# Turned softmax blocks of a decoder layer: sixteen SBUF-to-SBUF moves per unit, or four stores to DRAM and one fetch

## The chip, the cores and the metric

One NeuronCore of one Trainium2 chip runs the whole layer. The metric is device time in microseconds (us) of one execution. Stages are found by their time from the start of the profiled span.

## What is computed

A post-norm decoder layer over x (32 sequences of 56 tokens, 256 features): self-attention, cross-attention over 1500 context rows of 128 features per sequence, and a mixture-of-experts feed-forward part. The change lies in cross-attention alone:

```python
q = (text_hidden @ Wq).reshape(B, T_text, N_HEADS, HEAD_DIM).transpose(0, 2, 1, 3)    # 16 heads of 128
k = (vision_tokens @ Wk) ...  ; v = (vision_tokens @ Wv) ...                          # 8 heads, repeated twice
scores = jnp.einsum('bhtd,bhsd->bhts', q, k) / scale      # here 16*56 = 896 rows by 1500 keys per sequence
attn = jax.nn.softmax(jnp.where(mask, scores, -jnp.inf), axis=-1)
out = jnp.einsum('bhts,bhsd->bhtd', attn, v)
return out.transpose(0, 2, 1, 3).reshape(B, T_text, N_HEADS * HEAD_DIM) @ Wo
```

All is float32. A float32 product is made of three matmuls on a rounded part and a rest (`_hi`, `_lo`), so each operand is split by a rounding copy (ScalarE) and a subtraction (VectorE or GpSimd).

## The kernel before, in words

Three stages follow each other: `phase_a` (self-attention and queries, up to about 200 us), `phase_b` (cross-attention, up to about 2020 us, line 650 on), `phase_c` (experts). Keys and values are folded into the query and output weights ahead, so in `phase_b` the context itself serves as keys (`cT_*`, 128 x 1500) and as values (`c_*`, 125 partitions of 12 rows).

A batch m is one of the 32 sequences. Its 896 rows are seven units of 128 rows. For each unit TensorE makes three score fills of 500 keys (L860 to L862), VectorE takes each fill into `p` with the mask and a running maximum (L1070, then L1079), ScalarE makes the exponentials of the unit (L977). To multiply by the values the probabilities must be turned, so that keys lie on partitions. This is done in two ways:
- the three odd units by TensorE: 12 steps, one per column group c: turn (L874), round (`p_round`, L960), rest (`p_rest`, L1095), weigh (`weigh_odd`, L893 to L895);
- the four even units by VectorE and DMA: `turn_blocks` (L1090) transposes a unit in blocks of 32 x 32 into `by_block` (two buffers, unit u uses u % 2), and `move_blocks` on SyncE's queue (L799 to L808) brings the blocks into `keyed`, where row 32 r + j holds the keys. A unit takes sixteen DMAs of 32 partitions x 1536 bytes, one for each pair (a, r) of a partition strip a of `by_block` and a partition strip r of `keyed`. Then come 12 steps in two halves of six (units 0 and 1, then 2 and 3): round (`keyed_round` on ScalarE, L970), rest (`keyed_rest` on GpSimd, L1247, written over `keyed`), weigh (`weigh_even`, L916 to L918).

The order of work is written out by hand. Every engine goes through the same step number n = 0 to 23 (`STEPS`) of each batch, and work of a later stage lags by a fixed number of steps. The points that matter: `turn_blocks` of units 0 to 3 at `BLOCKS_AT` = 5, 8, 13, 17; `keyed_round` at steps 19 to 30 (`EVEN_HI`), so that the first half begins at step 19 and the second at step 25, which is step 1 of the next batch; weighing of even units two steps later; odd units turned at steps 31 to 42, which are 7 to 18 of the next batch. Step n + 24 of batch m is step n of batch m + 1. Score banks, turn banks and `pT_hi` are three deep, so the engines can't run far apart. Every second batch also holds a projection of two sequences (L928, four steps) with a norm (`norm`, `norm_out`) and the store of `y2`.

Waits around the change: `keyed_round` waits at the start of each half for the DMAs of its two units; `turn_blocks(m, u)` waits until the DMAs of the unit that had the same `by_block` buffer have landed; the moves of units 0 and 2 wait until the half of `keyed` that they overwrite has been weighed (`pv_done`). SyncE's queue is in order and carries also the loads of q (`load_q`), of the context in both forms (`load_cT`, `load_c`), of the mask, and the residual and `y2`. ScalarE's queue carries `store_rden` (L984, the softmax denominators as single floats, at steps 16 and 26) and `load_rden` (L992, at steps 23 and 33), which waits for the former to land. `phase_c` writes over `by_block` and waits first for `attention.moved`.

Of the kernel before, what the change touches and what calls it, by code (L numbers as in the profile page):

```python
# [29 lines left out]
F32 = mybir.dt.float32  # L30
# [6 lines left out]
B, S, F = 32, 56, 256  # L37
# [13 lines left out]
QUADS = 4  # L51
ACROSS = 32 * CH
# [579 lines left out]
def phase_b(nc, D, semaphore, edge, opening, M_hi, M_lo, q_in, cT_in, ident, const_loaded):  # L632
    with ExitStack() as ctx:
        def sb(name, shape, dt=F32):
            edge[name] = -(-nc.sbuf_base // 32) * 32
            return ctx.enter_context(nc.sbuf_tensor("b_" + name, shape, dt))
# [5 lines left out]
        def sem(name):  # L642
            return semaphore("b_" + name)
# [11 lines left out]
        keyed = sb("keyed", [128, EVEN * QUADS, ACROSS])  # L655
# [3 lines left out]
        p = [None, sb("p1", [128, ODD, CTX])]  # L659
# [23 lines left out]
        by_block = sb("by_block", [128, 2, QUADS, CH, 32])  # L683
        p[0] = sb("p0", [128, EVEN_DEEP, CTX_PAD])
        edge["end"] = nc.sbuf_usable_end // 32 * 32
        half = nc.alloc_sbuf_tensor_at("b_half", [PAIR, 1], F32, offset=edge["end"])
# [9 lines left out]
        shift_done, exp_done = sem("shift_done"), sem("exp_done")  # L696
        turned, hi_done, lo_done, pv_done = sem("turned"), sem("hi_done"), sem("lo_done"), sem("pv_done")
        blocks_turned, keyed_lo_done, keyed_lo_last = sem("blocks_turned"), sem("keyed_lo_done"), sem("keyed_lo_last")
        keyed_loaded = [sem(f"keyed_loaded{u}") for u in range(EVEN)]
        rden_done, rden_stored, rden_loaded = sem("rden_done"), sem("rden_stored"), sem("rden_loaded")  # L700
        oT_done, oT_hi_done, oT_lo_done, proj_done = sem("oT_done"), sem("oT_hi_done"), sem("oT_lo_done"), sem("proj_done")
        z_done, stat_chain, var_done, rstd_done, y2_done = sem("z_done"), sem("stat_chain"), sem("var_done"), sem("rstd_done"), sem("y2_done")
# [8 lines left out]
        EVEN_HI = 19  # L711
        EVEN_PV, ODD_HI = EVEN_HI + 2, EVEN_HI + CH
        ODD_PV = ODD_HI + 2
        BLOCKS_AT = (5, 8, 13, 17)
        RDEN_AT, STORE_AT, LOAD_AT = (15, STEPS + 1), (16, STEPS + 2), (STEPS - 1, STEPS + 9)
        SCALE_AT = (EVEN_PV + CH - 1, ODD_PV + CH - 1)
        ROUND_AT, ROUND_REST_AT = SCALE_AT[1] + 1, SCALE_AT[1] + 2
# [1 line left out]
        CT_HI_AT, C_HI_AT, FIRST_SPLIT_AT = 4, 9, 12  # L719
        OT_OPS = 2  # L720
        TAIL = range(STEPS, ROUND_REST_AT + 1)
        MOVES = 16 * QUADS * QUADS
        ORDER = [(u, j) for u in range(EVEN) for j in range(FILLS)] + [
            (EVEN + u, j) for u, j in ((0, 0), (0, 1), (1, 0), (1, 1), (2, 0), (0, 2), (1, 2), (2, 1), (2, 2))]

# [33 lines left out]
        def row(m, u):  # L759

            return p[0][:, (EVEN * m + u) % EVEN_DEEP, :] if u < EVEN else p[1][:, u - EVEN, :]

        def whole(m):

            return STEPS * (m + 1)
# [3 lines left out]
        def keyed_part(tensor, half, first, count):  # L769


            return tensor[0:CK, GROUPS * half:GROUPS * (half + 1), 32 * first:32 * (first + count)]

        def by_blocks(ap, width):
            return ap.rearrange("p (g j) -> p g j", j=width)

        def sync(sp):
            def load_q(m):
                sp.wait_ge(q_split, 2 * m)
                sp.dma_start(q_in[:], D["q"][:, m]).then_inc(q_loaded, 16)  # L780

            def load_cT(m):
                sp.wait_ge(cT_lo_done, m)
                sp.dma_start(cT_in[:], D["ctxT"][m]).then_inc(cT_loaded, 16)

            def load_mask(m):
                if m:
                    sp.wait_ge(mask_ready, m)
                sp.dma_start(mask_in[:], D["mask"][m].partition_broadcast(128)).then_inc(mask_loaded, 16)

            def load_c(m):
                if m >= 2:
                    sp.wait_ge(pv_done, whole(m - 2))
                if m:
                    sp.wait_ge(c_loaded, 16 * m)
                sp.dma_start(c_raw[m % 2][:], D["ctx"][m]).then_inc(c_loaded, 16)

            def move_blocks(m, u):


                if m and u % 2 == 0:
                    sp.wait_ge(pv_done, STEPS * (m - 1) + CH // 2 * (u // 2 + 1))
                sp.wait_ge(blocks_turned, EVEN * m + u + 1)
                for a in range(QUADS):
                    for r in range(QUADS):
                        sp.dma_start(keyed[32 * r:32 * (r + 1), QUADS * u + a, :],  # L806
                                     by_block[32 * a:32 * (a + 1), u % 2, r].rearrange("q b j -> q (b j)")).then_inc(
                                         keyed_loaded[u], 16)  # L808

            def residual(i):  # L810

                sp.dma_start(z[:], D["y1"][:, i, :]).then_inc(res_loaded, 16)

            def store(i):
                sp.wait_ge(y2_done, i + 1)
                sp.dma_start(D["y2"][PAIR * i:PAIR * (i + 1), :], y2[:]).then_inc(y2_stored, 16)

            def load_ahead():
                load_mask(0)
                load_c(0)  # L820

            store_last_part, wait_stored = opening.sync(sp, load_ahead)
            load_q(1)
            load_cT(1)
            load_mask(1)
            for part in range(len(opening.stored)):
                store_last_part(part)
            wait_stored()
            residual(0)

            for m in range(B):
                move_blocks(m, 0)
                if m + 2 < B:
                    load_q(m + 2)
                move_blocks(m, 1)
                if m % 2 and m >= 3:
                    store((m - 3) // 2)
                    residual((m - 1) // 2)
                move_blocks(m, 2)
                if m + 2 < B:  # L840
                    load_cT(m + 2)
                    load_mask(m + 2)
                move_blocks(m, 3)
                if m < LAST:
                    load_c(m + 1)
            return lambda: store(END)
# [108 lines left out]
        def scalar(act):  # L955
# [6 lines left out]
            def keyed_round(m, s):  # L962

                n, half, pair = STEPS * m + s, s // (CH // 2), s % (CH // 2)
                if pair == 0:
                    for u in (2 * half, 2 * half + 1):
                        act.wait_ge(keyed_loaded[u], MOVES * (m + 1))
                if n >= 3:
                    act.wait_ge(pv_done, n - 2)
                act.copy(by_blocks(pT_hi[:, s % 3, :], 64), keyed_part(keyed, half, 2 * pair, 2)).then_inc(hi_done, 1)  # L970
# [45 lines left out]
            def lag_step(m, n):  # L1016
                if at := behind(m, n, ODD_HI, CH):
                    p_round(*at)
                if at := behind(m, n, EVEN_HI, CH):
                    keyed_round(*at)  # L1020
                for par in range(2):
                    if at := behind(m, n, LOAD_AT[par]):
                        load_rden(at[0], par)
                    if at := behind(m, n, STORE_AT[par]):
                        store_rden(at[0], par)
                if at := behind(m, n, ROUND_AT):
                    oT_round(at[0])
# [26 lines left out]
        def vector(dve):  # L1054
# [27 lines left out]
            def turn_blocks(m, u):  # L1082


                dve.wait_ge(exp_done, PUNITS * m + u + 1)
                if m or u >= 2:
                    dve.wait_ge(keyed_loaded[(u + 2) % EVEN], MOVES * (m + u // 2))
                own = row(m, u)
                keys = bass.AP(own.tensor, own.offset, [own.ap[0], [32, QUADS], [CK, CH], [1, 32]])
                dve.transpose(by_block[:, u % 2], keys).then_inc(blocks_turned, 1)  # L1090
# [92 lines left out]
            def block_step(m, n):  # L1183
                if n in BLOCKS_AT:
                    turn_blocks(m, BLOCKS_AT.index(n))

# [22 lines left out]
        def gpsimd(pool):  # L1209
# [60 lines left out]

        return Attention(
            sync, tensor, scalar, vector, gpsimd, edge, TAIL,
            q_split=(q_split, 2 * B), cT_split=(cT_lo_done, B),
            fill_done=(fill_done, PFILLS * B), fill_taken=(fill_taken, PFILLS * B),
            moved=[(loaded, MOVES * B) for loaded in keyed_loaded], rden_stored=(rden_stored, 32 * B),
            first_batch_weighed=(pv_done, whole(LAST - 1)), weighed=(pv_done, whole(LAST)),
            keyed_weighed=(pv_done, STEPS * LAST + CH), scaled=(oT_done, OT_OPS * 2 * B),
            projected=(proj_done, NPAIR), z_taken=(z_done, NPAIR), y2_stored=y2_stored)
# [931 lines left out]
def decoder_layer(nc, D):  # L2210
    with ExitStack() as ctx:
        def semaphore(name):
            return ctx.enter_context(nc.semaphore(name))

        with ExitStack() as memory:
            edge = {}

            def sb(name, shape, dt=F32):
                edge[name] = nc.sbuf_base
                return memory.enter_context(nc.sbuf_tensor(name, shape, dt))  # L2220

            ident_loaded = semaphore("ident_loaded")
            M_hi, M_lo = sb("M_hi", [128, XH, F], F32R), sb("M_lo", [128, XH, F], F32R)
            q_in, cT_in = sb("q_in", [128, ROWS]), sb("cT_in", [128, CTX])
            ident = sb("ident", [128, 128])
            opening = phase_a(nc, D, semaphore, M_hi, M_lo, q_in, cT_in, ident, ident_loaded)
            attention = phase_b(nc, D, semaphore, edge, opening, M_hi, M_lo, q_in, cT_in, ident, ident_loaded)
        phase_c(nc, D, semaphore, attention, ident)
# [68 lines left out]
```

## Time and profile before

| quantity | value |
|---|---|
| median of 2 runs | 2253.15 us (2252.69 to 2253.62) |
| the profiled execution | 2257.55 us, its span 2255.7 us |
| TensorE's mean granted clock over the span | 0.881 of full speed |
| busy over the span | PE 1710.5 us (76%), VectorE 1246.3 us (55%), ScalarE 1030.6 us (46%), GpSimd 1001.7 us (44%) |
| DMA | 241.19 MB, mean 107 GB/s |

The span goes from the first to the last instruction of the profiled execution; the 1.85 us between it and the execution's own time lie outside of it. Engines are PE (TensorE matmul), DVE (VectorE), ACT (ScalarE), POOL (GpSimd) and SP (SyncE); "SPq" and "ACTq" are the instructions with which these issue DMAs. Issuing is not counted as busy time. Times are us from the start of the span unless marked ns.

### The profile page before, as it was taken

The numbers are of one execution on the slowest core, as the hardware profiler recorded it, in microseconds if no ns is written. First come the engines' busy times: TensorE is split into PE (matmuls) and PEld (weight loads), VectorE is DVE, ScalarE is ACT, GpSimd is POOL, SyncE is SP. The second block draws the span as 40 slices with busy tenths as digits, with TensorE's granted clock in tenths as the row PEclk, the third lists the DMA queues.
The fourth block names the chain that finished last, engine by engine and source line by source line (L and its number), as shares of the span: only waits on it lengthen the run. The fifth ranks groups of instructions, "written<-read, shape, count | busy, mean of one in ns | idle before, by whom it ended". The sixth has DMA issues, their size and how long they took to land.

```text
span 2255.7 us, 30072 instructions
## 1 busy us (share of the span) xinstructions
PE 1710.5 (76%) x9650; PEld 1533.9 (68%) x9650; DVE 1246.3 (55%) x3160; ACT 1030.6 (46%) x1780; POOL 1001.7 (44%) x700
## 2 busy tenths in 40 slices
PE   8996667677777777777776777776777777768997
PEld 7895556676667666666666666666666666658896
DVE  6554455555555555555655555545565655555647
ACT  5433444444444444444544454434454544444452
POOL 1112444444444444454544454535454545443525
PEclk9998888888888888888888888888888888989999
DMA  4345434444344444343444344434444434343233
GB/s 158 107 136 172 105 101 101 107 100 111 100 112 102 109 103 100 100 110 103 109 104 105 102 109 103 105 96 110 103 109 105 107 101 108 80 109 114 62 104 98
DMA packets 201175, 241.19 MB, mean 107 GB/s; under 512 B 69790, under 2 KB 180032, under 8 KB 200896
## 3 DMA queue, kind: packets, MB, share of 16 engines
q1 hardware_dynamic: 159088, 216.26, 35.9%
q10 hardware_dynamic: 38912, 14.80, 3.5%
q0 software_dynamic: 3024, 8.26, 1.3%
q8 instruction: 76, 1.25, 0.4%
q14 instruction: 75, 0.61, 0.1%
HBM read 113.62 MB, written 24.89 MB: 61 GB/s over the span
## 4 chain that ended last, share of the span: by engine, by line
SPq 56%; PE 24%; DVE 6%; issue 5%; DMA 5%; POOL 2%; ACT 2%; ACTq 0%; POOLq 0%; DVEq 0%
SPq L806 53%; PE a_bank L348 4%; DMA b_keyed<-b_by_block 3%; PE b_out L928 3%; POOL b_keyed_over L1247 2%; PE b_out L916 2%; DVE b_by_block L1090 2%; PE c_gate L1646 1%; PE b_score L860 1%; PE b_score L861 1%; PE b_score L862 1%; PE b_out L917 1%; PE b_out L918 1%; PE c_down L1673 1%; PE a_bank L374 1%
## 5 line engine op out<-in xcount | busy, mean ns | idle before, releaser
L1247 POOL TENSOR_TENSOR b_keyed_over<-b_keyed,b_pT_hi 125x512 fp32r<-125x512 f32 x378 | 496.1, 1332 | 904.5 <-ACT b_pT_hi L970 895.1
L1070 DVE CUSTOM_DVE_ANT_0 b_p<-b_score,b_mask_add 128x500 f32<-128x500 f32 x672 | 449.1, 668 | 474.7 <-PE b_score L862 470.0
L970 ACT CAST b_pT_hi<-b_keyed 125x512 fp32r<-125x512 f32 x384 | 224.9, 613 | 584.0 <-DMA b_keyed<-b_by_block 471.4
L893 PE MATMUL b_out<-b_pT_hi,b_c_hi 125*128 125x384 f32 x384 | 171.9, 448 | 317.8 <-DVE b_pT_lo L1095 317.8
L1090 DVE STREAM_TRANSPOSE b_by_block<-b_p 128x1536 f32<-128x1536 f32 x128 | 227.1, 1774 | 320.2 <-DMA b_keyed<-b_by_block 320.2
L977 ACT ACTIVATE b_p<-b_p,b_shift 128x1500 f32<-128x1500 f32 x224 | 346.7, 1548 | 88.7 <-DVE b_top_min L1079 88.4
L916 PE MATMUL b_out<-b_pT_hi,b_c_hi 125*128 125x256 f32 x768 | 254.0, 331 | 160.7 <-POOL b_keyed_over L1247 154.4
L960 ACT CAST b_pT_hi<-b_turn 125x384 fp32r<-125x384 f32 x384 | 182.3, 476 | 315.6 <-PE b_turn L874 313.8
L893 PEld LDWEIGHTS b_out<-b_pT_hi,b_c_hi 125*128 125x128 f32 x384 | 76.9, 200 | 346.2 <-DVE b_pT_lo L1095 344.8
L916 PEld LDWEIGHTS b_out<-b_pT_hi,b_c_hi 125*128 125x128 f32 x768 | 169.9, 221 | 202.0 <-POOL b_keyed_over L1247 183.4
L860 PE MATMUL b_score<-b_cT_hi,b_q_hi 128*128 128x500 f32 x672 | 286.5, 426 | 25.4 <-DVE b_top L1070 25.4
L861 PE MATMUL b_score<-b_cT_lo,b_q_hi 128*128 128x500 f32 x672 | 282.3, 420 | 0.0
L862 PE MATMUL b_score<-b_cT_hi,b_q_lo 128*128 128x500 f32 x672 | 280.8, 418 | 0.0
L917 PE MATMUL b_out<-b_keyed_over,b_c_hi 125*128 125x256 f32 x768 | 237.7, 309 | 0.0
L918 PE MATMUL b_out<-b_pT_hi,b_c_raw_over 125*128 125x256 f32 x768 | 237.2, 309 | 0.0
L1095 DVE TENSOR_TENSOR b_pT_lo<-b_turn,b_pT_hi 125x384 fp32r<-125x384 f32 x384 | 209.6, 553 | 29.9 <-ACT b_pT_hi L960 29.7
L874 PEld LDWEIGHTS b_turn<-ident,b_p 128*125 128x125 f32 x1152 | 185.7, 190 | 24.2
L874 PE MATMUL b_turn<-ident,b_p 128*125 128x128 f32 x1152 | 191.6, 276 | 0.0
L917 PEld LDWEIGHTS b_out<-b_keyed_over,b_c_hi 125*128 125x128 f32 x768 | 169.1, 220 | 11.8
L918 PEld LDWEIGHTS b_out<-b_pT_hi,b_c_raw_over 125*128 125x128 f32 x768 | 166.4, 217 | 0.0
L862 PEld LDWEIGHTS b_score<-b_cT_hi,b_q_lo 128*128 128x128 f32 x672 | 140.4, 209 | 30.7
L860 PEld LDWEIGHTS b_score<-b_cT_hi,b_q_hi 128*128 128x128 f32 x672 | 141.5, 211 | 26.8 <-DVE b_top L1070 26.3
(261 smaller groups left out, 3380.0 us busy)
## 6 DMA issues: line engine op xcount, KB each, us to landing
b_keyed<-b_by_block SPq DMA_DIRECT2D x2048, 48.0 KB, 2.4
cT_in<-in_ctxT SPq DMA_DIRECT2D x32, 750.0 KB, 4.6
b_c_raw<-in_ctx SPq DMA_DIRECT2D x32, 750.0 KB
q_store<-a_fold_in_or_q_stage SPq DMA_DIRECT2D x16, 896.0 KB, 4.1
q_in<-q_store SPq DMA_DIRECT2D x32, 448.0 KB, 4.0
b_rden_all<-rden_store ACTq DMA_DIRECT2D x32, 256.0 KB, 3.8
b_rden_all<-rden_store ACTq DMA_DIRECT2D x32, 192.0 KB, 4.3
b_mask_in<-in_mask SPq DMA_DIRECT2D x32, 187.5 KB, 4.9
```

The source lines that it names most:

```text
L806: sp.dma_start(keyed[32 * r:32 * (r + 1), QUADS * u + a, :], by_block[32 * a:32 * (a + 1), u % 2, r].rearrange("q b j -> q (b j)")).then_i ...
L860: pe.matmul(out, q_hi[b][:, rows], cT_hi[b][:, keys], start=True, stop=False)
L861: pe.matmul(out, q_hi[b][:, rows], cT_lo[b][:, keys], start=False, stop=False)
L862: pe.matmul(out, q_lo[b][:, rows], cT_hi[b][:, keys], start=False, stop=True).then_inc(fill_done, 1)
L874: mm = pe.transpose(turn_bank[c % 3][0:CK, u * 128:(u + 1) * 128], p[1][:, u, c * CK:(c + 1) * CK], ident[:])
L916: pe.matmul(out, hi, own_hi, start=(c == 0 and half == 0), stop=False, skip_group_check=True)
L917: pe.matmul(out, hi, own_lo, start=False, stop=False, skip_group_check=True)
L918: mm = pe.matmul(out, lo, own_hi, start=False, stop=(c == CH - 1 and half == 1), skip_group_check=True)
L977: act.activation(own, own, ACT.Exp, bias=shift[:, par, k:k + 1], scale=float(X_SCALE), accum_out=den[:, par, k:k + 1]).then_inc(exp_done, 1)
L1070: dve.tensor_tensor_reduce(out=row(m, u)[:, keys], in0=score_bank[f % FILLS][:, 0:FW], in1=mask_add[:, b, keys], scale=1.0, scalar=-3.0e38 ...
L1090: dve.transpose(by_block[:, u % 2], keys).then_inc(blocks_turned, 1)
L1247: pool.tensor_tensor(keyed_part(keyed_lo, *part), keyed_part(keyed, *part), by_blocks(pT_hi[:, s % 3, :], 64).bitcast(F32), ALU.subtract). ...
```

## The change

A DRAM tensor `p_store` of [unit, r, i, a, 384] floats is added. `move_blocks` is split in two. `store_blocks` writes each partition strip a of `by_block` (32 partitions x 4 pieces of 1536 bytes) in one DMA, four DMAs per unit, in such an order that in DRAM a row of `keyed` is contiguous. `load_keyed` fetches a unit with one DMA of 128 partitions x 6144 bytes. `by_block` is free when the stores have landed (`p_stored`), no longer when `keyed` is filled. The fetches are queued behind the stores of the following unit, the third and fourth turning go from steps 13 and 17 to 12 and 15, and the other loads are placed anew between them.

```diff
-        keyed_loaded = [sem(f"keyed_loaded{u}") for u in range(EVEN)]
+        p_stored = [sem("p_stored_even"), sem("p_stored_odd")]
+        keyed_loaded = [sem("keyed_loaded_first"), sem("keyed_loaded_last")]
-        BLOCKS_AT = (5, 8, 13, 17)
+        BLOCKS_AT = (5, 8, 12, 15)
-        MOVES = 16 * QUADS * QUADS
+        STORES, LOADS = 16 * QUADS, 16 * 2
-            def move_blocks(m, u):
-                if m and u % 2 == 0:
+            def store_blocks(m, u):
+                sp.wait_ge(blocks_turned, EVEN * m + u + 1)
+                if m:
+                    sp.wait_ge(keyed_loaded[u // 2], LOADS * m)
+                for a in range(QUADS):
+                    sp.dma_start(D["p"][u, :, :, a].rearrange("r i n -> i r n"),
+                                 by_block[32 * a:32 * (a + 1), u % 2].rearrange("q r b j -> q r (b j)")).then_inc(
+                                     p_stored[u % 2], 16)
+            def load_keyed(m, u):
+                if m:
                     sp.wait_ge(pv_done, STEPS * (m - 1) + CH // 2 * (u // 2 + 1))
-                sp.wait_ge(blocks_turned, EVEN * m + u + 1)
-                for a in range(QUADS):
-                    for r in range(QUADS):
-                        sp.dma_start(keyed[32 * r:32 * (r + 1), QUADS * u + a, :],
-                                     by_block[32 * a:32 * (a + 1), u % 2, r].rearrange("q b j -> q (b j)")).then_inc(
-                                         keyed_loaded[u], 16)
+                sp.wait_ge(p_stored[u % 2], STORES * (2 * m + u // 2 + 1))
+                sp.dma_start(keyed[:, QUADS * u:QUADS * (u + 1), :],
+                             D["p"][u].rearrange("r i a n -> (r i) a n")).then_inc(keyed_loaded[u // 2], 16)
             for m in range(B):
-                move_blocks(m, 0)
+                store_blocks(m, 0)
                 if m + 2 < B:
                     load_q(m + 2)
-                move_blocks(m, 1)
+                store_blocks(m, 1)
+                load_keyed(m, 0)
+                store_blocks(m, 2)
+                load_keyed(m, 1)
                 if m % 2 and m >= 3:
                     store((m - 3) // 2)
                     residual((m - 1) // 2)
-                move_blocks(m, 2)
                 if m + 2 < B:
                     load_cT(m + 2)
+                store_blocks(m, 3)
+                if m + 2 < B:
                     load_mask(m + 2)
-                move_blocks(m, 3)
+                load_keyed(m, 2)
+                load_keyed(m, 3)
                 if m < LAST:
                     load_c(m + 1)
-                    for u in (2 * half, 2 * half + 1):
-                        act.wait_ge(keyed_loaded[u], MOVES * (m + 1))
+                    act.wait_ge(keyed_loaded[half], LOADS * (m + 1))
-                    dve.wait_ge(keyed_loaded[(u + 2) % EVEN], MOVES * (m + u // 2))
+                    dve.wait_ge(p_stored[u % 2], STORES * (2 * m + u // 2))
-            moved=[(loaded, MOVES * B) for loaded in keyed_loaded], ...
+            moved=[(stored, STORES * 2 * B) for stored in p_stored], ...
```

## Rows read from the trace of the kernel before

**Rows 1.** The chain that ended last, by line, from the page:

```profile
SPq L806 53%; PE a_bank L348 4%; DMA b_keyed<-b_by_block 3%; PE b_out L928 3%; POOL b_keyed_over L1247 2%; PE b_out L916 2%; DVE b_by_block L1090 2%; PE c_gate L1646 1%; PE b_score L860 1%; PE b_score L861 1%; PE b_score L862 1%; PE b_out L917 1%; PE b_out L918 1%; PE c_down L1673 1%; PE a_bank L374 1%
```

**Rows 2.** SyncE's queue over one batch (start us, us, what):

```profile
1115.97 10.76 SPq L806 DMA_DIRECT2D b_keyed<-b_by_block  x16
...
1127.40 20.81 SPq L806 DMA_DIRECT2D b_keyed<-b_by_block  x32
1148.25 0.58 SPq L784 DMA_DIRECT2D cT_in<-in_ctxT  x1
...
1149.35 10.01 SPq L806 DMA_DIRECT2D b_keyed<-b_by_block  x16
1159.46 0.43 SPq L796 DMA_DIRECT2D b_c_raw<-in_ctx  x1
1172.93 10.25 SPq L806 DMA_DIRECT2D b_keyed<-b_by_block  x16
```

**Rows 3.** VectorE in order of time, [idle before it <- what ended it]:

```profile
1114.12 1.78 DVE L1090 STREAM_TRANSPOSE b_by_block<-b_p 128x1536 f32<-128x1536 f32 x1
...
1128.14 1.78 DVE L1090 STREAM_TRANSPOSE b_by_block<-b_p 128x1536 f32<-128x1536 f32 x1 [1.47 <-DMA b_keyed<-b_by_block]
...
1142.82 1.78 DVE L1090 STREAM_TRANSPOSE b_by_block<-b_p 128x1536 f32<-128x1536 f32 x1 [8.89 <-DMA b_keyed<-b_by_block]
...
1171.08 1.78 DVE L1090 STREAM_TRANSPOSE b_by_block<-b_p 128x1536 f32<-128x1536 f32 x1
...
1202.88 1.78 DVE L1090 STREAM_TRANSPOSE b_by_block<-b_p 128x1536 f32<-128x1536 f32 x1 [10.37 <-DMA b_keyed<-b_by_block]
```

**Rows 4.** ScalarE in order of time, the first rounding of a half:

```profile
1105.97 0.62 ACT L970 CAST b_pT_hi<-b_keyed 125x512 fp32r<-125x512 f32 x1 [6.65 <-DMA b_keyed<-b_by_block]
...
1142.79 1.14 ACT L970 CAST b_pT_hi<-b_keyed 125x512 fp32r<-125x512 f32 x2 [7.92 <-DMA b_keyed<-b_by_block]
...
1160.79 0.62 ACT L970 CAST b_pT_hi<-b_keyed 125x512 fp32r<-125x512 f32 x1 [6.62 <-DMA b_keyed<-b_by_block]
...
1221.24 0.62 ACT L970 CAST b_pT_hi<-b_keyed 125x512 fp32r<-125x512 f32 x1 [6.40 <-DMA b_keyed<-b_by_block]
```

**Rows 5.** Line 1090 alone over the whole span: first and last start, its idle time:

```profile
L1090 DVE STREAM_TRANSPOSE b_by_block<-b_p x128: 1760/1778/1780, 193.2 to 1994.1; 128x1536 f32<-128x1536 f32 x128
...
  DMA b_keyed<-b_by_block: 320.2, 49
```

**Rows 6.** Costliest groups, the one of line 970 (idle before it, releaser):

```profile
L970 ACT CAST b_pT_hi<-b_keyed 125x512 fp32r<-125x512 f32 x384 | 224.9, 613 | 584.0 <-DMA b_keyed<-b_by_block 471.4
```

**Rows 7.** DMA issues: count, KB each, median us from issue to landing:

```profile
b_keyed<-b_by_block SPq DMA_DIRECT2D x2048, 48.0 KB, 2.4
cT_in<-in_ctxT SPq DMA_DIRECT2D x32, 750.0 KB, 4.6
...
slot_store<-c_y2T SPq DMA_DIRECT2D x35, 128.0 KB, 1.7
...
rden_store<-b_rden ACTq DMA_DIRECT2D x32, 2.0 KB, 9.3
rden_store<-b_rden ACTq DMA_DIRECT2D x32, 1.5 KB, 13.4
```

**Rows 8.** Stretches: us, busy PE, PEld, DVE, ACT, POOL, granted clock, DMA share, GB/s:

```profile
1130.00:1147.00 17.00, 7.06 (x34) 6.26 (x35) 7.92 (x21) 2.64 (x6) 2.49 (x2) 0.80 0.39 83
...
1108.00:1115.90 7.90, 7.90 (x39) 7.33 (x40) 3.23 (x7) 5.62 (x7) 6.11 (x5) 0.68 0.32 59
1161.00:1172.00 11.00, 9.20 (x59) 8.83 (x60) 2.37 (x7) 6.45 (x10) 6.57 (x6) 0.84 0.30 58
...
15.00:22.00 7.00, 7.00 (x56) 6.03 (x55) 4.19 (x8) 2.90 (x12) 0.57 (x1) 1.00 1.05 438
```

**Rows 9.** The same columns, for a batch without and a batch with a projection:

```profile
1104.00:1158.80 54.80, 39.38 (x216) 35.58 (x217) 29.05 (x77) 26.71 (x41) 27.35 (x17) 0.84 0.42 107
1158.80:1219.20 60.40, 44.28 (x249) 39.44 (x247) 34.21 (x86) 26.73 (x41) 27.89 (x18) 0.86 0.40 100
```

More of the change, by code:

```diff
@@ L1274, in phase_b @@
             fill_done=(fill_done, PFILLS * B), fill_taken=(fill_taken, PFILLS * B),
-            moved=[(loaded, MOVES * B) for loaded in keyed_loaded], rden_stored=(rden_stored, 32 * B),
+            moved=[(stored, STORES * 2 * B) for stored in p_stored], rden_stored=(rden_stored, 32 * B),
             first_batch_weighed=(pv_done, whole(LAST - 1)), weighed=(pv_done, whole(LAST)),
@@ L2290 @@
     D["rden"] = nc.dram_tensor("rden_store", (B, 2, 128 * EVEN), F32, kind="Internal").ap()
+    D["p"] = nc.dram_tensor("p_store", (EVEN, QUADS, 32, QUADS, ACROSS), F32, kind="Internal").ap()
     D["y2"] = nc.dram_tensor("y2_store", (B * S, F), F32, kind="Internal").ap()
```

## The prediction, made before the changed kernel ran

> **What bounds the kernel now.** I read the chain of waits first. More than half of it is one line, L806, the issuing of the block moves on SyncE's queue [rows 1]. No compute engine is at its limit: in a batch PE is busy 39 to 44 us of 55 to 60 (at a granted clock of 0.84 to 0.86), VectorE 29 to 34, ScalarE and GpSimd 27 to 28 [rows 9]. Next I read SyncE's queue over one batch. The moves are issued back to back: 10.76 + 20.81 + 10.01 = 41.6 us for 64 of them, 0.65 us each; then the queue has nothing to issue but the context load until the next turning is done, at 1172.93 [rows 2].
>
> Then I looked at who is late because of it. VectorE stands 1.47 and 8.89 us in one batch and 10.37 us in the next before it may overwrite `by_block` [rows 3]. ScalarE stands 7.92 us at step 19, released at the same moment as VectorE's 8.89, and 6.62 and 6.40 us at step 25 [rows 4]. Over the span VectorE waits 320.2 us and ScalarE 471.4 us for these DMAs [rows 5, 6]; divided by 32 that is 10.0 and 14.7 us, so this pair of batches is typical. Waits that coincide count once: 1.47 + 8.89 + 6.62 = 17.0 us in the batch without a projection, 10.37 + 6.40 = 16.8 us in the one with it. The mean is 16.9 us per batch.
>
> The length of a batch: line 1090 starts first at 193.2 and last at 1994.1 [rows 5]. Within the last batch unit 3 is turned 31.8 us after unit 0 (1171.08 to 1202.88 in a batch of its kind, [rows 3]). So 31 batches take 1800.9 - 31.8 = 1769 us, 57.1 us each.
>
> **The change, part by part.**
>
> *Issuing.* Sixteen issues per unit become five. The price of an issue of 128 partitions is 0.58 us (`cT_in`, [rows 2]), that of a 32-partition one 0.65 us. Twenty issues cost about 13 us in place of 41.6. SyncE's queue stops being what the batch waits for, and 57.1 - 16.9 = 40.2 us per batch is what the steps take when nobody stands for a block.
>
> *Refilling.* Part of these 40.2 us is recovery from the stand. After the wait at step 25 PE works the whole of 7.90 us at a granted clock of 0.68, and in the other batch 9.2 of 11 us at 0.84 [rows 8]. At the full clock the same work would be 2.5 and 1.8 us shorter. But here GpSimd also makes a rest per step, so I credit 1.5 us; the ends are 0 and 2.1.
>
> *The round trip.* Call T the start of unit 2's turning, at step 12 now. How fast do the stores drain? From 1130 to 1147 little but moves runs: 83 GB/s at a DMA share of 0.39, so 213 GB/s if it were full; loads of all partitions reach 438 GB/s at a full share [rows 8]. A store reads one strip of 32 partitions, as a move does. I take the moves' rate, 0.92 us for 192 KB and 3.7 us per unit; at the other rate it would be 0.45 us and 1.8. Here the Trainium skill has a rule, in "SBUF — State Buffer", section Door 1: the rate of a DMA depends on how many of the 16 SBUF ports its partitions reach, and a strip of 32 reaches half of them. By that rule, the trace's 213 against 438 agrees, and it holds for a store whose other side is DRAM; the sum would be by it as I have it, and without it 1.9 us per unit better.
> The fetch: `cT_in`, 750 KB, lands after 4.6 us [rows 7]; at 438 GB/s some 1.8 us of it are transfer, so 2.8 are fixed.
> Unit 1's fetch is issued behind unit 2's four stores. Turning 1.8, first issue 0.6, draining 3.7, transfer 1.8, the rest of the fetch's latency 1.8 (I take a third of the fixed part as hidden behind the queue): it lands at T + 9.7. It is needed at step 19. From step 13 (1128.14) ScalarE came to step 19 at 1142.79 - 7.92 = 1134.87 [rows 3, 4], 6.7 us; with one step more (1.3) and unit 3's turning, which now lies ahead of step 19 (1.8), it needs it at T + 9.8. That is even; as both sides are good to some 1.5 us I charge 0.7. Bounds: 0 and 3.
> Unit 3 is turned at step 15, which ends at T + 6.3. In the queue ahead of its stores are that fetch and `cT_in` (to T + 10.1). Stores drain to T + 13.8 and land at T + 15.3; unit 2's fetch lies behind them, and unit 3's is issued at T + 15.9 and lands 4.3 later, T + 20.2. The second half is needed at step 25: one step 1.3, steps 13 to 17 in 1142.82 - 8.89 - 1128.14 = 5.8, steps 17 to 25 in 1160.79 - 6.62 - 1142.82 = 11.4 [rows 3, 4], sum T + 18.5. Charge 1.7 us; bounds 0 and 5 (all fixed parts in full, stores queued behind a context load).
>
> *The landing of the stores.* Does DRAM land later than SBUF? The Trainium skill says in "DMA: Bandwidth & Descriptors", Anatomy of one DMA, that the semaphore waits for the write receipt and HBM is the heaviest target; that speaks against this change. The nearest row is `slot_store`, 128 KB to DRAM in 1.7 us, below the 2.4 us of a 48 KB move in a full queue [rows 7]. The row does not bear it out at this size, and I charge nothing more.
>
> *Denominators.* ScalarE's `load_rden` waits for a store that lands after a median of 9.3 us (issued at step 16, needed at 23) or 13.4 us (step 26, needed at 33) [rows 7]. Today seven steps with their stands cover it. From 1161 to 1172, while the second kind is in flight, the DMA share is 0.30 at 58 GB/s [rows 8]: the context load `b_c_raw`, issued at 1159.46, drains on few engines. In the new order it starts some steps earlier than the store. Seven unhindered steps are about 10 us. I charge 0.9 us; bounds 0 and 3.
>
> *The rest.* The moved turnings cost the same 1.78 us; units 2 and 3 have their exponentials at steps 10 and 13, so they find them. VectorE's wait for `by_block` now ends when unit u - 2 has been stored, at least seven steps back: nothing. Stores 0 and 1 have `load_q` between them, which waits for GpSimd's split, finished before unit 1 is turned: nothing. `load_cT` now stands before the stores of unit 3 and waits for GpSimd's rest of the previous one: done at step 11, nothing; if GpSimd is late, unit 3's stores and both fetches are late with it. Phase C waits for stores in place of moves: below 3 us, uncounted.
>
> *Sum per batch:* 40.2 - 1.5 + 0.7 + 1.7 + 0.9 = 42.0 us, 15.1 less than 57.1. Over 31 batches 468 us. The profiled execution took 2257.6 us, so 1789.6; the median of the runs lies 4.4 us below it: **1785 us**.
>
> **The rivals.**
>
> *The engines run closer still.* Everything that stands falls away and the clock stays up, so that PE sets the pace: 39.38 x 0.84 = 33.1 and 44.28 x 0.86 = 38.1 us at full clock, mean 35.6 [rows 9]; with about one us of friction 36.6, 20.5 x 31 = 636 us less: 1617. For: PE at 0.68 after each stand. Against: VectorE is busy without a gap from step 5 to 20, PE in the rest, so the two limits add rather than overlap. 10%.
>
> *The DMA engines become late.* Now 0.42 x 54.8 = 23 us of full share per batch; moves are 3.1 MB at 213 GB/s, 14.8. Stores cost the same, fetches 3.1 MB at 438 add 7.2: 30 us of 42. If this queueing puts each half another 3 us later than charged, a batch takes 48: 9.1 x 31 = 282 us less, 1971. For: 0.7 of the engines' time, 32-partition transfers in order. Against: the transfers have seven steps each. 10%.
>
> *Slower.* The four stores of a unit don't overlap each other and each takes its landing: 1.7 us for 128 KB [rows 7], 2.6 us for 192 KB. Sixteen are 41 us, on top of the 23 - 14.8 + 7.2 = 15.6 of the rest; to that comes the wait of unit 3's fetch for the last store, 4.6 us that nothing else fills: 61.6 us per batch, 4.5 x 31 = 140 more: 2393. It decides once a store takes over 2.3 us on the queues. Against: `slot_store` is one transfer alone, moves overlap in the same queue. 3%.
>
> *The wait only changes its name:* unit 3's round trip of 20 us grows to 35, so that a batch takes 57 again: 2253. 2%.
>
> **How the numbers follow.** The forecast has 75%, the rivals 10, 10, 3 and 2. Range: 39 us per batch gives 2253 - 561 = 1692, 46.3 us gives 1918, so 1690 to 1920; most of the first two rivals is outside. A measurement of this kernel can tell about 2% (45 us) from no change. Faster by more 0.95, within 0.02, slower 0.03.
>
> **What would show it.** Right: L806's successors gone from the chain, which is then shared by PE and VectorE; SyncE's queue issues below 15 us per batch; VectorE no longer idle before L1090; ScalarE idle before L970 for a fetch 1 to 3 us per batch; a median landing of 3 to 4 us for the stores and 4 to 6 for the fetches; batches of 38 to 40 and 44 to 46 us; a granted clock above 0.9 in phase B. Wrong: a store landing after over 5 us, ScalarE idle over 5 us per half, or SyncE's queue standing before `load_cT` while unit 3 is turned.

## The result and the profile after

The changed kernel takes 1969.69 us (median of two runs, 1965.54 and 1973.85) against 2253.15: a ratio of 0.874, 95% interval 0.866 to 0.882. It is faster, as forecast, but by 283 us in place of 468, and lies outside of the range (1690 to 1920). The profiled execution has a span of 1963.7 us.

First the page of the changed kernel: busy times, the chain that ended last by line, the group of `keyed_round`, and the DMA issues with their landing.

```profile
PE 1650.7 (84%) x9650; PEld 1488.7 (76%) x9650; DVE 1224.5 (62%) x3160; ACT 1030.9 (52%) x1780; POOL 999.6 (51%) x700
...
DMA b_keyed<-p_store 16%; DMA p_store<-b_by_block 7%; DVE b_by_block L1101 6%; PE b_out L940 4%; PE a_bank L348 4%; DVE b_p L1081 4%; SPq L805 4%; PE b_out L928 3%; POOL b_keyed_over L1258 3%; ACT b_pT_hi L981 3%; ACT b_p L988 3%; PE b_out L929 3%; PE b_out L930 3%; DVE b_pT_lo L1106 3%; PE b_score L872 2%
...
L981 ACT CAST b_pT_hi<-b_keyed 125x512 fp32r<-125x512 f32 x384 | 228.7, 614 | 376.6 <-DMA b_keyed<-p_store 274.1
...
p_store<-b_by_block SPq DMA_DIRECT2D x512, 192.0 KB, 3.7
b_keyed<-p_store SPq DMA_DIRECT2D x128, 768.0 KB, 7.0
cT_in<-in_ctxT SPq DMA_DIRECT2D x32, 750.0 KB, 12.6
```

Issuing is gone from the head of the chain (L806 had 53% [rows 1], L805 has 4%), and PE and VectorE have moved up. But DMA now has 16 + 7% of it, in flight and not being issued. ScalarE still waits 274.1 us for blocks, 8.6 us per batch; before it was 471.4 [rows 6]. The load of the context for the scores (`cT_in`, 750 KB), which landed after 4.6 us [rows 7], takes 12.6.

VectorE's turning has hardly any wait left, against 320.2 us [rows 5]:

```profile
L1101 DVE STREAM_TRANSPOSE b_by_block<-b_p x128: 1740/1770/1779, 193.6 to 1698.6; 128x1536 f32<-128x1536 f32 x128
...
  DMA p_store<-b_by_block: 10.1, 2
```

Worked as in the prediction (a last batch with a projection turns unit 3 some 18.9 us after unit 0, as from 1011.32 to 1030.23), a batch takes (1505.0 - 18.9) / 31 = 47.9 us, where 1505.0 is the time from the first to the last turning. Forecast were 42.0; before it was 57.1.

Where does the block come from so late? SyncE's queue over one batch of the changed kernel:

```profile
1027.68 2.04 SPq L805 DMA_DIRECT2D p_store<-b_by_block  x4
1029.83 0.71 SPq L814 DMA_DIRECT2D b_keyed<-p_store  x1
...
1031.90 0.52 SPq L785 DMA_DIRECT2D cT_in<-in_ctxT  x1
1032.52 2.19 SPq L805 DMA_DIRECT2D p_store<-b_by_block  x4
1034.75 0.48 SPq L790 DMA_DIRECT2D b_mask_in<-in_mask  x1
1035.33 12.55 SPq L814 DMA_DIRECT2D b_keyed<-p_store  x2
```

The last line is two fetches; between them SyncE stands for unit 3's stores. The chain of the same batch names it (start us, us, what):

```profile
1034.27 13.23 DMA p_store<-b_by_block
1047.56 6.38 DMA b_keyed<-p_store
1053.96 0.63 ACT b_pT_hi L981
```

The wait is not always in this half. In this batch ScalarE waits 0.66 us at step 19 and 4.39 at step 25; in most batches the longer wait is at step 19, as in the one before:

```profile
990.79 1.14 ACT L981 CAST b_pT_hi<-b_keyed 125x512 fp32r<-125x512 f32 x2 [6.53 <-DMA b_keyed<-p_store]
```

Stores of 192 KB that land after 3.7 us in the median take 13.2 here. What else happened then stands in ScalarE's row of 1032.02, and the stretches show what the DMA engines did (us, busy PE, PEld, DVE, ACT, POOL, granted clock, DMA share, GB/s):

```profile
1032.02 0.39 ACTq L995 DMA_DIRECT2D rden_store<-b_rden  x1
```

```profile
1034.00:1036.00 2.00, 2.00 (x13) 1.80 (x12) 1.59 (x4) 0.56 (x2) 0.00 (x0) 1.00 1.01 354
1036.00:1038.00 2.00, 2.00 (x12) 1.83 (x11) 1.49 (x6) 1.71 (x3) 1.01 (x1) 1.00 1.39 340
1038.00:1046.00 8.00, 6.71 (x43) 5.70 (x42) 4.55 (x16) 4.98 (x8) 5.32 (x5) 1.00 1.01 118
1046.00:1048.00 2.00, 0.94 (x6) 0.48 (x4) 0.24 (x2) 0.58 (x1) 0.00 (x0) 1.00 0.89 305
```

For 8 us the DMA engines are booked in full on average and move 118 GB/s, a third of what they move just before. This begins 6 us after ScalarE has issued the store of the softmax denominators, 512 single floats. So two theories:
- *Narrow writes:* the store of single floats to DRAM slows all that is in flight with it.
- *Queue:* the fetches are late because they stand in order behind stores and loads in SyncE's queue.

### The profile page after: what moved, and what is told of

The parts are those of the page before. It is cut to its first block, busy times and chain, and to the rows that moved or that the text cites. A ratio compares the mean times of both kernels' runs of the same rounds, so it can differ in the third digit from the quotient of the medians.

```text
span 1963.7 us, 28846 instructions
## 1 busy us (share of the span) xinstructions
PE 1650.7 (84%) x9650; PEld 1488.7 (76%) x9650; DVE 1224.5 (62%) x3160; ACT 1030.9 (52%) x1780; POOL 999.6 (51%) x700
## 4 chain that ended last, share of the span: by engine, by line
PE 36%; DMA 25%; DVE 18%; ACT 8%; SPq 5%; POOL 4%; issue 3%; DVEq 0%; POOLq 0%; ACTq 0%
DMA b_keyed<-p_store 16%; DMA p_store<-b_by_block 7%; DVE b_by_block L1101 6%; PE b_out L940 4%; PE a_bank L348 4%; DVE b_p L1081 4%; SPq L805 4%; PE b_out L928 3%; POOL b_keyed_over L1258 3%; ACT b_pT_hi L981 3%; ACT b_p L988 3%; PE b_out L929 3%; PE b_out L930 3%; DVE b_pT_lo L1106 3%; PE b_score L872 2%
## 5 line engine op out<-in xcount | busy, mean ns | idle before, releaser
L981 ACT CAST b_pT_hi<-b_keyed 125x512 fp32r<-125x512 f32 x384 | 228.7, 614 | 376.6 <-DMA b_keyed<-p_store 274.1
L928 PEld LDWEIGHTS b_out<-b_pT_hi,b_c_hi 125*128 125x128 f32 x768 | 167.3, 218 | 266.6 <-issue 175.9
L988 ACT ACTIVATE b_p<-b_p,b_shift 128x1500 f32<-128x1500 f32 x224 | 346.5, 1547 | 23.2 <-DMA rden_store<-b_rden 13.7
L872 PE MATMUL b_score<-b_cT_hi,b_q_hi 128*128 128x500 f32 x672 | 275.9, 411 | 11.6 <-DVE b_top L1081 11.6
L874 PE MATMUL b_score<-b_cT_hi,b_q_lo 128*128 128x500 f32 x672 | 273.1, 406 | 0.0
L873 PE MATMUL b_score<-b_cT_lo,b_q_hi 128*128 128x500 f32 x672 | 272.7, 406 | 0.0
L1101 DVE STREAM_TRANSPOSE b_by_block<-b_p 128x1536 f32<-128x1536 f32 x128 | 226.0, 1766 | 10.1 <-DMA p_store<-b_by_block 10.1
L905 PE MATMUL b_out<-b_pT_hi,b_c_hi 125*128 125x384 f32 x384 | 160.8, 419 | 38.8 <-DVE b_pT_lo L1106 38.8
L874 PEld LDWEIGHTS b_score<-b_cT_hi,b_q_lo 128*128 128x128 f32 x672 | 134.3, 200 | 28.3
L872 PEld LDWEIGHTS b_score<-b_cT_hi,b_q_hi 128*128 128x128 f32 x672 | 134.2, 200 | 13.3 <-DVE b_top L1081 12.7
L873 PEld LDWEIGHTS b_score<-b_cT_lo,b_q_hi 128*128 128x128 f32 x672 | 135.8, 202 | 0.6
## 6 DMA issues: line engine op xcount, KB each, us to landing
cT_in<-in_ctxT SPq DMA_DIRECT2D x32, 750.0 KB, 12.6
```

The lines of the kernel that those rows point to most:

```text
L872: pe.matmul(out, q_hi[b][:, rows], cT_hi[b][:, keys], start=True, stop=False)
L873: pe.matmul(out, q_hi[b][:, rows], cT_lo[b][:, keys], start=False, stop=False)
L874: pe.matmul(out, q_lo[b][:, rows], cT_hi[b][:, keys], start=False, stop=True).then_inc(fill_done, 1)
L928: pe.matmul(out, hi, own_hi, start=(c == 0 and half == 0), stop=False, skip_group_check=True)
L988: act.activation(own, own, ACT.Exp, bias=shift[:, par, k:k + 1], scale=float(X_SCALE), accum_out=den[:, par, k:k + 1]).then_inc(exp_done, 1)
```

## Experiments

All kernels below start from the changed kernel except where said. Ratios are to the kernel before, from runs beside it.

### Wider denominator writes

```diff
-                act.dma_start(D["rden"][m, par, 0:128 * u].rearrange("(u q) -> q u", q=128),
-                              rden[:, par, 0:u], allow_slow_non_contiguous=True)...
+                act.dma_start(D["rden"][m, par, 0:128 * u].rearrange("(q u) -> q u", q=128),
+                              rden[:, par, 0:u])...
```

> The changed kernel with the denominators stored as 128 pieces of 16 (or 12) bytes in place of 512 (or 384) single floats; their order in DRAM is another, so they scale other columns. Two theories of why each half of keyed comes 4 to 8 us later than forecast. Narrow writes: whatever is in flight when the 512 single-float writes of step 16 arrive waits 8 to 10 us for them; then ScalarE's idle time before L981 falls from 274 us to under 100 and the time to 1780-1850. Queue: the fetch is late because it stands behind stores and loads in one queue; then nothing but ScalarE's 13.7 us of waits for the denominators goes, 1950-1975.

The denominators now lie in DRAM in another order, so this kernel, like all below that have this pattern, scales wrong columns: it shows a time and is no replacement. Measured: 1785.87 us, ratio 0.793 (0.791 to 0.795). One DMA pattern, with 3.5 KB of each batch's bytes (2.0 and 1.5 KB), is worth 184 us. ScalarE's wait for blocks in this kernel (us in total, times, longest), and its DMA issues:

```profile
ACT b_pT_hi L981 <- DMA b_keyed<-p_store: 135.2, 54, 19.9
```

```profile
b_keyed<-p_store SPq DMA_DIRECT2D x128, 768.0 KB, 6.8
cT_in<-in_ctxT SPq DMA_DIRECT2D x32, 750.0 KB, 7.8
```

135.2 us where there were 274.1 is over the "under 100" expected; the time is what narrow writes predict, and queue is out as the main cause. The same place of a batch in this kernel, 8 us begun 6 us after the denominator store of 1023.99, against the 118 GB/s above:

```profile
1030.00:1038.00 8.00, 6.71 (x41) 5.69 (x40) 4.53 (x15) 7.75 (x12) 6.24 (x6) 1.00 0.95 351
```

Nearly the same share, and 351 GB/s. Narrow writes themselves leave hardly a trace: in the 8 slow microseconds of the changed kernel ScalarE's queue (q10), which carries them, has a share of 1.7%, SyncE's (q1) 98.8%:

```profile
q1 hardware_dynamic: 613, 0.94, 98.8%
q10 hardware_dynamic: 190, 0.00, 1.7%
```

The time is booked on the others' packets.

### The order of the queue, with narrow writes

```diff
                 load_keyed(m, 0)
+                load_keyed(m, 1)
                 store_blocks(m, 2)
-                load_keyed(m, 1)
+                load_keyed(m, 2)
...
                 store_blocks(m, 3)
...
-                load_keyed(m, 2)
                 load_keyed(m, 3)
```

> The changed kernel with unit 1's fetch queued ahead of unit 2's stores and unit 2's fetch ahead of unit 3's. Queue: unit 1's fetch lands before step 12 is over, the waits of 6 to 8 us at step 19 go, most of 274 us: 1780-1850. Narrow writes: the fetch of unit 1 lands before the writes of step 16 too, so the first half's wait goes here as well, but unit 3's stores and fetch are then hit and the second half's wait grows: 1850-1930, with ScalarE's idle time before L981 moved to step 25 rather than gone.

Measured: 2064.96 us, ratio 0.918 (0.916 to 0.921): 95 us slower than the changed kernel, which neither theory had. SyncE's queue and ScalarE's wait at step 25:

```profile
1034.11 2.65 SPq L805 DMA_DIRECT2D p_store<-b_by_block  x4
1046.36 0.34 SPq L814 DMA_DIRECT2D b_keyed<-p_store  x1
1046.74 0.43 SPq L785 DMA_DIRECT2D cT_in<-in_ctxT  x1
1047.27 2.28 SPq L805 DMA_DIRECT2D p_store<-b_by_block  x4
```

```profile
1060.54 0.62 ACT L981 CAST b_pT_hi<-b_keyed 125x512 fp32r<-125x512 f32 x1 [10.20 <-DMA b_keyed<-p_store]
```

The wait has moved from step 19 to step 25, as narrow writes say. It has grown because SyncE now stands 9.6 us for unit 2's stores (1036.76 to 1046.36) with unit 3's stores queued behind it, although VectorE had turned that unit at 1038.4. A fetch placed right behind its own stores turned their landing into a stop for the whole queue.

### The denominators three steps later

```diff
-        RDEN_AT, STORE_AT, LOAD_AT = (15, STEPS + 1), (16, STEPS + 2), (STEPS - 1, STEPS + 9)
+        RDEN_AT, STORE_AT, LOAD_AT = (15, STEPS + 1), (19, STEPS + 2), (STEPS + 1, STEPS + 9)
```

> The changed kernel with the even denominators stored at step 19 in place of 16 and fetched at 25 in place of 23; nothing else. Narrow writes: the wait at step 19 (6 to 8 us in most batches) shrinks to under 2 us and the one at step 25 grows to 5 us or more; the time moves by less than 3% either way. Queue: both waits stay as they are, step 19 at 6 to 8 us, time within 1% of 1970.

Measured: 1967.51 us, ratio 0.874. ScalarE's waits at steps 19 and 25 in one batch:

```profile
1037.32 0.62 ACT L981 CAST b_pT_hi<-b_keyed 125x512 fp32r<-125x512 f32 x1 [2.63 <-DMA b_keyed<-p_store]
...
1053.14 0.62 ACT L981 CAST b_pT_hi<-b_keyed 125x512 fp32r<-125x512 f32 x1 [7.17 <-DMA b_keyed<-p_store]
```

In the batches between 1000 and 1300 us step 19 waits 2.0 to 3.5 us (I had said under 2) and step 25 waits 6.1 to 8.0: the harm follows the store from the first half to the second. The time, as expected, doesn't tell the theories apart; the place of the wait does.

### The kernel before, with wider denominator writes

> The kernel before with the same wider denominator writes as in the first run. Both theories: the batch is set by issuing 64 moves, so the time stays within 1% of 2253. Narrow writes: the moves' landing falls from 2.4 us a little and up to 1 us per batch is won at the tail of a half, down to 2220.

The edit is that of the first run, on the kernel before. Measured: 2236.03 us, ratio 0.992 (0.990 to 0.995). VectorE's wait before the turning falls from 320.2 to 172.9 us, but ScalarE's for blocks stays (471.4 and 469.3) and the total hardly moves, since the batch is held by issuing. The same store that costs 184 us of the changed kernel costs 16 to 18 of the old one: there its harm was hidden by the bottleneck that the change removed.

### Unit 1 fetched early, without narrow writes

The first run with `load_keyed(m, 1)` alone moved ahead of `store_blocks(m, 2)`.

> The first run (16-byte denominator writes, denominators in another order) with unit 1's fetch queued ahead of unit 2's stores. If, without narrow writes, the rest of ScalarE's idle time before L981 (115 us) comes from unit 1's fetch standing behind unit 2's stores, then the waits at step 19 go and the time falls by 30 to 80 us from 1786, to 1710-1755. If the queue's order is no matter, 1775-1795.

Measured: 1772.82 us, ratio 0.788 (0.786 to 0.790) against 0.793 (0.791 to 0.795) of the first run: about 13 us, less than half of the least expected. SyncE stands for stores more often, but never long (at L813 76 times, 4.9 us at most, 210.2 us in all against 137.1). ScalarE waits fewer times for blocks (37 in place of 54), but hardly less in sum (126 us, 135 before).

### Only the odd denominators wider

The wider pattern for `par` = 1 (step 26), single floats kept for `par` = 0 (step 16).

> The changed kernel with only the odd denominators (step 26) in wide writes, in another order; the even ones (step 16, 512 single floats) stay narrow. Narrow writes, with the even ones doing the harm because they meet the stores and fetches of both halves: most of the 184 us between 1970 and 1786 is still there, 1920-1970. If the odd ones at step 26, which meet only the context load, cost as much: about 1880.

Measured: 1949.11 us, ratio 0.865 (0.860 to 0.869). Of the 184 us the odd store has about 21, which is hardly clear of the noise (the changed kernel has 0.866 to 0.882), and the even one about 163, 131 of it in ScalarE's wait for blocks (265.9 us in this kernel, 135.2 in the first run). The likely reason is what is in flight beside each: stores, a context load and a fetch at step 16, mostly the context load `b_c_raw` at step 26. No run moves the one store to the other's place.

### The context load on more DMA engines

```diff
-                sp.dma_start(c_raw[m % 2][:], D["ctx"][m]).then_inc(c_loaded, 16)
+                for rows in (slice(0, 112), slice(112, CK)):
+                    sp.dma_start(c_raw[m % 2][rows], D["ctx"][m, rows]).then_inc(c_loaded, 16)
```

(on the first run, with the counts of `c_loaded` doubled)

> The first run with the context load of 125 partitions (L797) as two DMAs of 112 and 13 partitions. It drains on few DMA engines now (share 0.30 for 12 us). If that holds up the stores of the next batch's first units or the odd denominators, 10 to 40 us are won: 1745-1775. If nothing waits for those few engines, 1780-1792.

Measured: 1796.12 us, ratio 0.801 (0.797 to 0.804): 10 us slower than the first run, if anything. Nothing that bounds the batch waited for those few engines, although the odd denominators, in flight beside that load, now land after 3.1 us in place of 5.8.

### The denominators turned, in full

This version computes all of the reference. `rden` becomes 32 wide, VectorE transposes it in 32 x 32 blocks, and each of the four (three) units is stored in one DMA of 4 partitions x 128 bytes, in the old order:

```diff
+                dve.transpose(rden_T[:, par, :], rden[:, par, :]).then_inc(rden_done, 1)
...
-                act.dma_start(D["rden"][m, par, 0:128 * u].rearrange("(u q) -> q u", q=128), rden[:, par, 0:u], ...
+                for k in range(u):
+                    act.dma_start(D["rden"][m, par, 128 * k:128 * (k + 1)].rearrange("(a j) -> a j", j=32),
+                                  rden_T[k::32, par, :]).then_inc(rden_stored, 16)
```

> The changed kernel, computing the reference in full, with the denominators transposed by VectorE in 32 x 32 blocks and stored in pieces of 128 bytes, 16 (or 12) pieces in four (or three) DMAs of 4 partitions. Narrow writes: the gain of the first run comes back but for ScalarE's five more issues per batch (about 1.9 us of its queue, mostly hidden) and VectorE's two small transposes (0.2 us): 1785-1830. Queue: 1960-1990.

Measured: 1791.08 us, ratio 0.797 (0.795 to 0.800). The gain is there with all values in place, for seven DMAs per batch in place of two.

### Single floats put back, for nothing

```diff
+                if par == 0:
+                    act.dma_start(D["spare"][0:512].rearrange("(u q) -> q u", q=128), rden[:, 0, 0:4],
+                                  allow_slow_non_contiguous=True).then_inc(rden_stored, 16)
```

> The turned-denominators kernel (1791 us) with one more DMA per batch, whose result nobody uses: the 512 even denominators at step 16 as single floats into a DRAM tensor of its own. Narrow writes: the cost is back although the kernel no longer needs them, 1930-1980. If the gain came from the denominators landing sooner for ScalarE and not from the harm to others, 1791-1830 (ScalarE still waits for this DMA at step 23, so its own wait is seen apart).

Measured: 2008.83 us, ratio 0.894 (0.891 to 0.896), 218 us more than the run before: above the range. Its waits:

```profile
ACT b_pT_hi L982 <- DMA b_keyed<-p_store: 208.7, 64, 22.2
ACT b_p L989 <- DMA spare_store<-b_rden: 140.1, 31, 6.1
```

So 140 us are ScalarE's own wait for the added store's landing, and 67 (208.7 against 142.0 us) the blocks'. By ScalarE's waits the larger part is not harm to others here; the run is weaker than I meant it. In the changed kernel it is the other way round: ScalarE waits 13.7 us in all for the store, and the blocks cost 139 us more than with wider writes. The two waits are not independent prices, as while ScalarE stands for the one, the other goes on landing. The rate of the DMA engines is clearer. Eight us begun 4 to 5 us after the last of ScalarE's even stores, in the run before and in this one:

```profile
1036.00:1044.00 8.00, 6.68 (x42) 5.41 (x41) 4.34 (x14) 6.97 (x11) 6.33 (x6) 1.00 0.92 333
...
1061.00:1069.00 8.00, 5.45 (x33) 4.61 (x34) 3.11 (x9) 5.72 (x9) 6.13 (x5) 1.00 1.22 127
```

The added 2 KB bring the rate back down from 333 to 127 GB/s.

### Number or width

The added DMA writes 512 pieces of 16 bytes: `D["spare"].rearrange("(u q w) -> q u w", q=128, w=4)` from `rden[:, 0, 0:16]`.

> As the run before, but the added DMA writes 512 pieces of 16 bytes in place of 512 of 4. If the number of small pieces costs, it is as slow as that run, 1930-1980. If the width of a float costs, it stays near 1791-1830. The first run had both changed at once (128 pieces of 16 bytes).

Measured: 1847.16 us, ratio 0.822 (0.819 to 0.825): 56 us for 512 pieces of 16 bytes, 218 for as many of 4. Neither clean case came. The number costs something, and four bytes a piece cost nearly four times as much as sixteen. But most of that difference is ScalarE's own wait for the landing, 1.2 us here against 140.1; its wait for blocks is 194.4 against 208.7 us, 52 and 67 above the kernel without the added store. The rate at the same place lies between the two above:

```profile
1074.00:1082.00 8.00, 6.45 (x41) 5.32 (x40) 4.29 (x16) 7.03 (x11) 6.15 (x6) 1.00 0.97 291
```

### Two orders of the queue, with turned denominators

> The turned-denominators kernel with unit 1's fetch queued ahead of unit 2's stores, in full: a version meant to beat both kernels. The pair with 16-byte writes gave 13 us; the same here: 1770-1785.

Measured: 1782.62 us, ratio 0.793 (0.791 to 0.795) against 0.797 (0.795 to 0.800) without the early fetch. It is the fastest full version of this study, 187 us below the changed kernel, though the step from 1791 is at the edge of what the intervals tell.

> The turned-denominators kernel with the queue order of the second run (units 1 and 2 fetched ahead of the next unit's stores), which with narrow writes cost 95 us (2065 against 1970). If that loss came from SyncE's queue standing for unit 2's stores while narrow writes held these up (12 us), it is gone: 1765-1800. If the order itself is bad, 1850-1900.

Measured: 1884.91 us, ratio 0.837 (0.835 to 0.839). My explanation of the second run fell in part: without narrow writes the order still costs 94 us. It needs no slow store to stop the queue:

```profile
946.63 3.00 SPq L806 DMA_DIRECT2D p_store<-b_by_block  x4
954.16 0.34 SPq L815 DMA_DIRECT2D b_keyed<-p_store  x1
954.54 0.43 SPq L786 DMA_DIRECT2D cT_in<-in_ctxT  x1
955.07 2.10 SPq L806 DMA_DIRECT2D p_store<-b_by_block  x4
...
965.10 0.34 SPq L815 DMA_DIRECT2D b_keyed<-p_store  x1
```

```profile
969.38 0.62 ACT L982 CAST b_pT_hi<-b_keyed 125x512 fp32r<-125x512 f32 x1 [6.60 <-DMA b_keyed<-p_store]
```

SyncE stands 4.5 us for unit 2's stores (949.63 to 954.16) and then 7.4 for unit 3's (957.71 to 965.10), in a row, because unit 3's are issued only after the first stand. SyncE's waits for stores at that line are 400.7 us in this kernel and 123.5 in the one it starts from. In the changed kernel's order the two round trips overlap. The last two runs differ in nothing but the place of unit 2's fetch, so that place alone costs 102 us (1885 against 1783).

## Why the prediction was wrong

*Right: the bottleneck and what is left without it.* The issuing of L806 held the batch, and 40.2 us less the 1.5 of *Refilling*, 38.7, was the forecast for steps in which nobody stands. Of the changed kernel's 47.9 us ScalarE stands 8.6 for blocks and 0.4 for denominators, which leaves 38.9. With wider writes the batch is (1530.1 - 194.1 - 18.9) / 31 = 42.5 us, and 42.5 - 4.2 = 38.3. The clock forecast held as well: 0.924 of full speed over the span, from 0.881, and 0.970 with wider writes; the forecast for phase B was above 0.9, and from 240 to 1700 us it is 0.92.

*Right: VectorE, SyncE, the stores.* VectorE's wait for `by_block` went (10.1 us in all); stores land after a median of 3.7 us (forecast 3 to 4); SyncE's queue issues four stores in 2.0 to 3.1 us.

*Wrong: the charges for the round trip, by what the step "Denominators" left out.* The batch is 5.9 us longer than the forecast. ScalarE's wait for blocks makes 6.2 of it: the sum charged 0.7 + 1.7 = 2.4 us for the two fetches, and they take 8.6. The denominators' own wait is 0.5 less than charged, the steps 0.2 more. In most batches ScalarE stands over 5 us at step 19, and the store above took 13.2 us to land: two of the prediction's signs of being wrong.

The larger part of these 6.2 us goes back to the step "Denominators". The prediction saw that their store lands after 9.3 and 13.4 us [rows 7] and asked only who waits for it: ScalarE, 0.9 us, bounds 0 and 3. That term was right in size (13.7 us in all, 0.4 per batch). What it never asked is what the store does to the DMAs beside it, and so put it at nothing. With wider writes a batch is 47.9 - 42.5 = 5.4 us shorter, more than all charges of the sum together (3.3 us), 4.4 of it in ScalarE's wait for blocks (8.6 to 4.2). Over 31 batches these are 169 of the 184 us; the rest lies outside of them, most of it behind the last turning. With that one pattern made wider the kernel takes 1786 us; 1785 was the forecast. That the two agree to a microsecond is luck: ScalarE's wait for blocks is then 4.2 us per batch where 2.4 were charged, and the denominators' 0.9 is gone. So the round trip was too short by 1.8 us even without narrow writes, and which of its parts was, no run shows.

The rows could have warned. The rate for stores was read from 1130 to 1147, 83 GB/s at a share of 0.39 [rows 8], without asking why that was a poor rate: the stretch holds a denominator store of 1131.54. Two stretches of 8 us with moves alone, begun 2.5 to 3 us after the even denominators' store, first of the kernel before and then of the same with wider denominator writes (columns as above):

```profile
1134.00:1142.00 8.00, 2.78 (x16) 2.20 (x14) 0.00 (x0) 0.48 (x1) 0.00 (x0) 0.89 0.43 78
...
1014.70:1022.70 8.00, 2.49 (x13) 1.92 (x11) 2.71 (x4) 1.62 (x3) 2.04 (x2) 0.98 0.30 80
```

That is 181 GB/s per full share beside single floats and 267 beside wider writes. The figure of 213, taken for a property of 32-partition strips, was in part the denominators' doing, and so was the closeness to a half that the prediction found in it. (The 438 GB/s beside it were at a share of 1.05, so 417 at a full one; that changes the transfer times by under 0.1 us.) Stores of the changed kernel, read where no denominators are in flight, also do better than 213:

```profile
1014.00:1016.50 2.50, 2.50 (x21) 2.38 (x20) 2.27 (x9) 0.86 (x2) 1.20 (x2) 1.00 0.94 232
```

247 GB/s per full share. It stays well below the mixed stretch of the first run, 351 at 0.95, so 369, and that strips of 32 partitions are slower is still the better reading.

*The rivals.* "The DMA engines become late" gave 1971 and the kernel takes 1970, but for another reason than argued. It rested on the queueing of 32-partition transfers, and all of these are still there in the kernel of 1786 us. The landing in DRAM as such didn't decide: the large stores land in 3.7 us in the median, as forecast. For it the Trainium skill ("DMA: Bandwidth & Descriptors", Anatomy of one DMA) calls HBM the heaviest target. The same page of the Trainium skill says, in Specifications, that below 512 bytes a transfer is carried out as read-modify-write. The runs agree that small writes cost more than their bytes. They also show that not all below that size are alike: 512 pieces of 16 bytes cost 56 us and as many of 4 bytes 218. That it is a read-modify-write which costs the time, no run shows.

## What to carry to other kernels

When a change makes a kernel lean on DMA in flight where before it leaned on issuing, look at every DMA that shares that time, also those nobody waits for: read each one's landing, and beside it GB/s per DMA share in stretches with and without it. A store of single floats spread over partitions is the first suspect, however few its bytes; turn it on chip into longer pieces. In an in-order queue put a fetch behind work that is due anyway, not right behind the stores it needs.

## What was not expected of the hardware

- A store of 512 single floats (2 KB) to DRAM makes each batch about 5 us longer (163 us in all), most of it by what it does to other DMAs: 118 GB/s at a full DMA share for 8 us, with the time booked on the other queue's packets (98.8% to 1.7%). Which part of the path is held was not found.
- The cost grows with narrowness at the same number of pieces: 56 us (16 bytes) against 218 us (4 bytes) over 32 batches, of which 140 are ScalarE's own wait for the landing. In the stretches shown the DMA engines move 291 GB/s beside the former, 127 beside the latter and 333 with neither.
- The context load of 125 partitions, which drains for 11 us and more at a share of 0.30 [rows 8], did not hold the batch: in two parts it brought nothing (1796 against 1786 us).
